# Row and router stages fused in five parts, a bf16 bias product, weights loaded a stage ahead, and stage ends without GpSimd's drain

## What is computed

```python
edge_index = jnp.stack([src, dst])
x = x + gnn0(layernorm(x), src, dst)          # x + segment sum of edge-weighted x[src], then bn_relu(h @ W + b) twice
x = x + ffn0(layernorm(x))                    # softmax router over 8 experts, top 2, layernorm, W1, gelu, W2
x = x + gnn1(layernorm(x), edge_index, w)     # two hconv: relu(x @ w1 + b1), segment_sum, @ w2 + b2, bn, relu
x = x + ffn1(layernorm(x))                    # shared mlp + 4 gated experts, top 2

def _hconv(x, src, dst, ew, w1, b1, w2, b2, g, b):
    h = jax.nn.relu(x @ w1 + b1)
    msg = ew[:, None] * h[src]
    agg = jax.ops.segment_sum(msg, dst, num_segments=x.shape[0])
    h = agg @ w2 + b2
    return jax.nn.relu(_bn(h, g, b))
```

## Time and profile before

| | us |
|---|---|
| runs | 5695.45, 5695.61, 5719.21 |
| median | 5695.61 |
| the profiled execution | 5692.53 |
| its span, first to last instruction | 5690.8 |
| TensorE busy in the span | 3907.4 (69%) |
| DVE, ACT, GpSimd busy | 2066.0, 1935.9, 3004.5 |
| TensorE's mean granted clock | 0.832 of 2.4 GHz |

### The profile page before, as it was taken

The page is one execution under the profiler, slowest core; times in us unless marked ns, Lnnn a source line. Parts: engine busy times, 40 slices in busy tenths (PEclk is TensorE's granted clock), DMA queues, the critical chain, the costliest instruction groups (busy, mean ns, idle before and its releaser), DMA issues. The chain is left out here.

```text
span 5690.8 us, 77820 instructions
## 1 busy us (share of the span) xinstructions
PE 3907.4 (69%) x16120; PEld 3044.7 (54%) x16121; DVE 2066.0 (36%) x5417; ACT 1935.9 (34%) x4772; POOL 3004.5 (53%) x2633
## 2 busy tenths in 40 slices
PE   2666666666577599999765565667555556664798
PEld 2555555555475488888544444446344445453665
DVE  5444444455456511111422222234422222336333
ACT  2222222223243222222243333333633333336422
POOL 2888888888800022222047777774277777760000
PEclk9777788888886799999777878888777787886699
DMA  6666666666640355555323333331233333320000
GB/s 225 88 88 88 88 89 88 88 88 88 82 145 0 132 181 191 177 192 177 124 89 101 102 102 102 101 101 50 85 101 101 102 101 102 102 79 0 15 22 19
DMA packets 353879, 568.89 MB, mean 100 GB/s; under 512 B 61598, under 2 KB 274460, under 8 KB 350993
## 3 DMA queue, kind: packets, MB, share of 16 engines
q0 software_dynamic: 198720, 337.81, 29.4%
q1 hardware_dynamic: 150820, 226.00, 12.1%
q10 hardware_dynamic: 4268, 4.30, 0.2%
HBM read 404.84 MB, written 163.07 MB: 100 GB/s over the span
## 5 line engine op out<-in xcount | busy, mean ns | idle before, releaser
L638 POOL DMA_INDIRECT T<-h_rows,segment_sum_idx x1568 | 1546.0, 986 | 727.3 <-issue 395.0
L674 PE MATMUL bank<-T 128*128 128x256 f32 x3904 | 1239.2, 481 | 811.8 <-PEq L69 811.1
L674 PEld LDWEIGHTS bank<-T 128*128 128x128 f32 x3904 | 916.3, 244 | 1134.1 <-issue 974.1
L392 POOL DMA_INDIRECT node_sums<-T,scattered_sum_idx x784 | 1214.3, 1549 | 343.8 <-issue 218.2
L654 ACT ACTIVATE T<-T,segment_sum_edge 128x256 f32<-128x256 f32 x1568 | 667.9, 496 | 1180.0 <-DMA T<-h_rows,segment_sum_idx 1180.0
L463 PE MATMUL bank<-X,T 128*128 x1952 | 631.9, 481 | 103.5 <-PEq L69 100.3
L457 PE MATMUL bank<-T 128*128 128x128 f32 x1952 | 342.2, 331 | 418.5 <-PEq L69 418.3
L701 DVE TENSOR_TENSOR A<-A,bank 128x256 f32 x488 | 205.2, 421 | 1110.0 <-DVEq L69 1109.8
L463 PEld LDWEIGHTS bank<-X,T 128*128 128x128 f32 x1952 | 462.8, 249 | 203.3 <-issue 125.9
L457 PEld LDWEIGHTS bank<-T 128*128 128x128 f32 x1952 | 300.7, 233 | 431.0 <-issue 426.6
L498 DVE SCALAR_TENSOR_TENSOR T<-T,edges,not_after 128x128 f32<-128x128 int16 x784 | 223.8, 348 | 543.9 <-DVEq L69 499.4
(11 more groups left out here) (285 smaller groups left out, 4759.2 us busy)
## 6 DMA issues: line engine op xcount, KB each, us to landing
T<-in_L_ffn_W SPq DMA_DIRECT2D x52, 1024.0 KB
A<-in_L_ffn_W SPq DMA_DIRECT2D x52, 1024.0 KB, 8.6
T<-src_lanes SPq DMA_DIRECT2D x196, 128.0 KB, 3.2
T<-h_rows,segment_sum_idx POOLq DMA_INDIRECT x1568, 2.7
node_sums<-A SPq DMA_DIRECT2D x3, 6528.0 KB, 33.5
A<-node_sums SPq DMA_DIRECT2D x36, 512.0 KB, 5.2
h_rows<-A SPq DMA_DIRECT2D x50, 256.0 KB, 2.1
node_sums<-T,scattered_sum_idx POOLq DMA_INDIRECT x784, 3.8
```

What stands on the lines that cost most here:

```text
L392: pool.indirect_dma_start(c.sum_dram[at % COPIES], bass.IndirectOffsetOnAxis(ap=idx[:, h % LR, j:j + 1], axis=0), msg[:, h % LR * G + j, : ...
L638: pool.indirect_dma_start(msg[:, h * G + j, :], None, c.h_dram, bass.IndirectOffsetOnAxis(ap=idx[:, h, j:j + 1], axis=0)).then_inc(landed[ ...
L674: mm = pe.matmul(acc[s][:, 0:D], hot[:, s, j, :], msg[:, h * G + j, :], start=(j == 0), stop=(j == G - 1))
```

## The change

1. `stage` opens its block with a flag that leaves out GpSimd's drain at the block's end. The clearing of semaphores and the barrier stay.
2. Two buffers `c.w` live through the program. Each `w` is loaded by SP in an earlier stage (`load_w`): two in scattered_sum, two in expert_ffn behind the first expert loads, one in each segment_sum. The product stages wait on counts of `c.w_in`.
3. combine_message makes the bias of a block with one product of 128x512 in bf16: the bias is split in three bf16 pieces on three partitions, all other partitions hold zero, and the other operand is all ones. Eight dependent DVE steps prepare it. From the third part on, a part's reciprocal and shift are taken in the middle of the next part.
4. norm_to_rows and router become one stage. `rows_in_parts` writes out the order of all 25 blocks in five parts (3, 5, 5, 6 and 6 blocks): "rows" of a block, then "sums", "root", and "turn". Logits are now made with the experts on the partitions, 256 nodes at a time, copied by ACT into a list and turned back by TensorE; ACT in place of DVE copies the turned block out of PSUM.

```diff
-        with nc.Block() as block:
+        with nc.Block(no_gpsimd_drain=True) as block:
...
+def load_w(eng, c, slot, w_dram):
+    eng.dma_start(c.w[slot][:], w_dram.rearrange("(k p) n -> p k n", p=P)).then_inc(c.w_in[slot], 16)
...
+def rows_in_parts():
+    blocks_of = [list(range(lo // 2, hi // 2)) for lo, hi in ROW_PARTS] + [[]]
+    order = [("rows", j) for j in blocks_of[0]] + [("sums", 0)]
+    for n in range(len(ROW_PARTS)):
+        here, later = blocks_of[n], blocks_of[n + 1]
+        order += [("rows", j) for j in later[:2]] + [("root", n)]
+        later = later[2:]
+        for u in range(max(len(here), len(later))):
+            order += [("turn", j) for j in here[u:u + 1]] + [("rows", j) for j in later[u:u + 1]]
+        if n + 1 < len(ROW_PARTS):
+            order.append(("sums", n + 1))
+    return order
...
+            def turn(n, j):
+                s = n % 2
+                if n == 0 or part_of_block(j) != part_of_block(turns[n - 1]):
+                    normalise(n)
+                take(act, turned[s])
+                if n + 1 < NJ and part_of_block(turns[n + 1]) == part_of_block(j):
+                    normalise(n + 1)
+                act.copy(in_cols(j), turn2[s][:].rearrange("p (k n) -> p k n", k=KD)).then_inc(back_ready[s], 1)
+                if n >= 1:
+                    keep_list(n - 1)
...
+            def turn_rows(n):
+                s = n % 2
+                take(pe, row_ready[s])
+                if n >= 1:
+                    logits_of(n - 1)
+                turn_to_cols(pe, c, row[s], turn2[s]).then_inc(turned[s], 1)
+                if n >= 2:
+                    lists_back(n - 2)
...
             def product(j):
...
+                pe.matmul(out[s][:], one[:], pieces[:].rearrange("p t d -> p (t d)"), start=True, stop=False, skip_group_check=True)
                 for q in range(2):
-                    at = out[s][:, q * D:(q + 1) * D]
-                    pe.matmul(at, one[:], bias[:], start=True, stop=False)
```

More of the change, by code:

```diff
@@ L1097, in norm_relu, with message_rows @@
     stage(nc, run, "norm_relu")
-def norm_to_rows(nc, c, residual):
+def message_rows(nc, c, w, w_ready, b_dram, from_x):
     def run(block, sb, sem):
[L1104 to L1146, removed]
-                        dve.scalar_tensor_tensor(x[:, q, :], x[:, q, :], c.mean[:, bass.ds(j * 2 + q, 1)], h[:, q, :],
-                                                 ALU.add, ALU.add).then_inc(v, 1)
-                    take(dve, v, 2)
-                dve.sem_inc(free[s], 1)
-                for q in range(2):
-                    stat_tile(dve, c, j * 2 + q)
-            blocks(dve, add)
-    stage(nc, run, "norm_to_rows")
@@ L1157, in message_rows @@
-def message_rows(nc, c, w_dram, b_dram, from_x):
-    def run(block, sb, sem):
-        w, bias = sb("w", [P, KD, D]), sb("bias", [P, D])
+        bias = sb("bias", [P, D])
         col = [sb(f"col{s}", [P, KD, BLK]) for s in range(2)]
@@ L1273, in router @@
     XC = 10
+    order = rows_in_parts()
+    turns = [j for kind, j in order if kind == "turn"]
     def run(block, sb, sem):
         wr, br = sb("wr", [P, KD, ne]), sb("br", [P, ne])
-        row = [sb(f"row{s}", [P, 2, D]) for s in range(2)]
         col = [sb(f"col{s}", [P, KD, BLK]) for s in range(2)]
+        sum_ = None if moe else [sb(f"sum{s}", [P, 2, D]) for s in range(2)]
+        lists = [carve(flat(c.A), 8400 + s * BLK, (BLK,))[0:ne] for s in range(2)]
+        row = [carve(flat(c.A), 9000 + s * 2 * D, (2, D)) for s in range(2)]
+        back = [carve(flat(c.A), 10100 + s * KD * BLK, (KD, BLK)) for s in range(2)]
         work = flat(c.T) if moe else flat(c.A)[:, NB * D // 2:]
         n3 = NB * ne
-        logit, prob, eid, cand, pick1, pick2 = (carve(work, i * n3, (NB, ne)) for i in range(6))
+        logit, prob, cand, pick1, pick2 = (carve(work, i * n3, (NB, ne)) for i in range(5))
+        eid = sb("eid", [P, NB, ne])[:]
         small = [carve(work, 6 * n3 + i * NB, (NB,)) for i in range(12)]
@@ L1349, in _, with cols_of @@
         def _(act):
-            root(act, go, done, c.rstd)
+            def cols_of(j):
+                s = j % 2
+                if j >= 2:
+                    take(act, cols_free[s])
+                if not moe:
+                    if j >= 2:
+                        take(act, sum_free[s])
+                    norm_block(act, c, sum_[s], j).then_inc(residual_ready[s], 1)
+                apply_affine(act, c, col[s], cols_block(c, j), ACT.Relu if moe else ACT.Identity).then_inc(cols_ready[s], 1)
@@ new lines, in keep_list, with normalise @@
+            def keep_list(n):
+                s = n % 2
+                take(act, lg_ready[s])
+                if n >= 2:
+                    take(act, list_free[s])
+                act.copy(lists[s], lg[s][0:ne, 0:BLK]).then_inc(list_ready[s], 1)
+            def normalise(n):
+                j = turns[n]
+                act.wait_ge(normed_to, part_of_block(j) + 1)
+                norm_block(act, c, row[n % 2], j).then_inc(row_ready[n % 2], 1)
+            def turn(n, j):
[8 more added lines that the diff above has]
+                    keep_list(n - 1)
@@ L1351, in _ @@
+            n = 0
+            for kind, j in order:
+                if kind == "rows":
+                    cols_of(j)
+                elif kind == "root":
+                    lo, hi = ROW_PARTS[j]
+                    root(act, go, done, c.rstd[:, lo:hi])
+                elif kind == "turn":
+                    turn(n, j)
+                    n += 1
+            keep_list(NJ - 1)
             if moe:
                 root(act, go, done, scale2)
-            take(act, stats_ready)
-            def norm(j, s):
-                take(act, row_free[s])
-                norm_block(act, c, row[s], j).then_inc(row_ready[s], 1)
@@ L1359, in to_t @@
-            def to_t(j, s):
-                take(act, in_t)
-                chain(act, act.copy(cols_block(c, j), col[s][:]), kept)
-                act.sem_inc(col_free[s], 1)
-            if moe:
-                blocks(act, norm)
-            else:
-                two_ahead(act, norm, to_t)
             take(act, exp_go)
@@ L1856, in _ @@
                     chain(dve, ins, v)
+                    if k == 0 and n >= 2:
+                        close(n - 1)
                 dve.sem_inc(y_free[r], 1)
```

237 lines of the change are left out of this document (149 added, 88 removed).

## The result

| | us |
|---|---|
| changed kernel, 4 runs | 5794.12 to 5808.46, median 5799.56 |
| kernel before, 4 runs | 5695.45 to 5719.21, median 5698.35 |
| ratio | 1.0171, 95% interval 1.0150 to 1.0192 |
| profiled execution | 5800.68, span 5798.9 |

A forecast was written before the change was run, and what follows sets the result against it. GpSimd's indirect DMAs and TensorE were taken to bound most of the span, untouched by the change. Fused stages +108, combine_message -20, weights -7.5, issues +0.5, drains -13.3: +67.7 on 5692.5, plus 3.1, gave 5763 us (range 5697 to 5800).

## What to carry to other kernels

When two loops are fused into one in-order program per engine, walk once round the loop by who waits for whom and add up the links; if the ring closes through both engines, its length is the sum and not the maximum of their work. In such a loop issue what does not hang on the awaited result ahead of the wait, and right behind the wait what the other engine needs first: here that alone was worth 135 us with no instruction added or taken away. And price a TensorE clock from what its long links will get, not from the mean of a stretch.

## What had not been expected

In some rounds the clock moved in step with the round. From 1840.4 us of the changed kernel, when the burst of one round is over, the granted clock is 1.00 for the pause and the transposes of the later block, which take 0.63 us as at 2.4 GHz; behind them it is 0.50 again, and the logits take 1.86 us; the same once more from 1847.2 on:

```profile
1849.81 0.63 PE L1404 MATMUL bank<-ident,router_col 128*128 128x128 f32 x4 [2.92 <-PEq L69]
...
1850.37 1.73 PE L1411 MATMUL bank<-A,router_wr 128*8 128x256 f32 x4
...
1840.40:1843.70 3.30, 0.59 (x5) 0.45 (x6) 0.00 (x0) 2.42 (x6) 0.00 (x0) 1.00 0.00 0
1843.80:1847.10 3.30, 3.09 (x10) 1.28 (x8) 1.62 (x4) 0.40 (x1) 0.00 (x0) 0.50 0.00 0
1847.20:1850.50 3.30, 0.69 (x5) 0.52 (x6) 0.00 (x0) 2.31 (x6) 0.00 (x0) 1.00 0.00 0
...
1912.00:1931.80 19.80, 10.64 (x59) 5.23 (x58) 0.18 (x1) 10.28 (x24) 0.00 (x0) 1.00 0.00 0
```

In the first stage this happens in these two rounds and once more at a part's end (transposes from 1862.6 us); in the other eleven rounds with a later block the clock stays at 0.50, in the round of 1811.88 too, and it stays up only from 1912.0 on, in rounds without a later block. Why one burst lifts the clock and the next, of the same work, does not is open. The Trainium skill (TensorE: Matmul & The Clock Gate, "HAM oscillation — how this bites in real kernels") tells of such a clock that swings with the pauses between groups of products; the trace agrees in those rounds. Two consequences were measured: work added into the pause made the kernel some 40 us faster, and shortening the pause by order alone brought the clock from 0.58 to 0.71 besides.
